# The value multiply of the edge sort on GpSimd instead of VectorE

## The reference

```
x = emb[x_ids]
for each layer:
    h = segment_sum(vals[:, None] * x[col], row)          # sparse times dense
    z = (h + x) @ Wa.T + ba + (h * x) @ Wb.T + bb
    x = where(z >= 0, z, 0.2 * z)
out = concatenate of x before the first layer and after each layer
```

## Time and profile before

| | |
|---|---|
| Median of 3 runs | 10225.11 us (10217.66 to 10225.59) |
| The profiled execution | 10220.25 us, span 10218.3 us |
| Busy share of the span | PE 90%, PE weight load 83%, VectorE 81%, GpSimd 50%, ScalarE 43% |
| Mean granted TensorE clock | 0.92 |
| Sort 0, about | 330 to 1731 us |
| Sort 1, about | 2080 to 3524 us |
| The three layers | from about 3750 us to the end |

### The profile page before, as it was taken

One profiled execution on the slowest core, in us unless ns is written; L12 is line 12 of the kernel. 1 busy time (PEld: TensorE's weight loads), 2 busy tenths in 40 slices (PEclk: granted clock), 3 DMA queues, 4 the chain that ended last, 5 costly groups with the idle time before them and its releaser, 6 DMA issues.

```text
span 10218.3 us, 236191 instructions
## 1 busy us (share of the span) xinstructions
PE 9241.7 (90%) x72184; PEld 8455.2 (83%) x72185; DVE 8226.2 (81%) x11648; ACT 4417.4 (43%) x13845; POOL 5098.6 (50%) x2843
## 2 busy tenths in 40 slices
PE   6788886788888669999999999999999999999999
PEld 4567665466676549999999999989999999999999
DVE  7899998699999857777777777777777777777777
ACT  0577775067777516652111256641111466511112
POOL 8477775057777500006888600028888200088885
PEclk8788887778888759999999999999999999999999
DMA  2111111011111299998888889998888699988885
GB/s 74 35 6 6 6 6 18 6 5 6 6 6 6 23 61 344 344 335 295 284 286 286 252 277 341 340 313 285 286 286 286 224 344 347 336 282 286 286 286 210
DMA packets 1121792, 1969.65 MB, mean 193 GB/s; under 512 B 390740, under 2 KB 442008, under 8 KB 1121080
## 3 DMA queue, kind: packets, MB, share of 16 engines
q0 software_dynamic: 399392, 1034.26, 32.8%
q1 hardware_dynamic: 722328, 934.52, 30.9%
HBM read 1212.58 MB, written 755.66 MB: 193 GB/s over the span
## 4 chain that ended last, share of the span: by engine, by line
PE 48%; DVE 20%; DMA 15%; issue 10%; ACT 3%; SPq 1%; DVEq 1%; POOL 0%; ACTq 0%; POOLq 0%
PE ps L912 35%; DMA messages<-work 14%; PE ps L903 7%; DVE hT L1102 7%; DVE place L1081 7%; DVE hT L1096 3%; ACT work L670 3%; PE ps L746 1%; PE ps L883 1%; PE ps L940 1%; PE ps L920 1%; PE ps L941 1%; PE ps L768 1%; DVE place L1086 0%; DVE place L1084 0%
## 5 line engine op out<-in xcount | busy, mean ns | idle before, releaser
L511 POOL DMA_INDIRECT work<-messages,work x1920 | 2923.1, 1522 | 3687.7 <-issue 3686.8
L912 PE MATMUL ps<-work 128*128 128x125 f32 x30720 | 3548.7, 278 | 38.3 <-DVE work L1279 38.3
L912 PEld LDWEIGHTS ps<-work 128*128 128x128 f32 x30720 | 3504.3, 192 | 82.7 <-DVE work L1279 39.4
L486 POOL DMA_INDIRECT sorted_edges<-stage,run_idx x798 | 1968.5, 2467 | 1286.1 <-ACT stage L615 570.9
L903 PE MATMUL ps<-xb,work 125*128 x21504 | 2459.2, 277 | 149.0 <-DVE work L1251 80.3
L903 PEld LDWEIGHTS ps<-xb,work 125*128 125x128 f32 x21504 | 2425.6, 193 | 182.6 <-issue 182.1
L1279 DVE TENSOR_TENSOR work<-work,iota_p 128x1000 f32<-128x1000 f32 x1920 | 2291.5, 1193 | 34.7 <-ACT work L688 34.7
L670 ACT ACTIVATE work<-ps,work 128x128 f32<-128x128 f32 x5376 | 1515.5, 372 | 1264.9 <-DMA messages<-work 648.5
L688 ACT ACTIVATE work<-work 128x8 f32<-128x8 f32 x1920 | 577.7, 301 | 2880.4 <-DMA work<-messages,work 2880.4
L796 PEld LDWEIGHTS ps<-hT 128*128 128x128 f32 x12768 | 1694.7, 215 | 69.4 <-issue 46.5
L626 ACT ACTIVATE hT<-iota_p,place 128x128 f32<-128x128 f32 x4788 | 1427.9, 386 | 707.7 <-DVE place L1086 699.7
(11 more groups left out here) (201 smaller groups left out, 3820.8 us busy)
## 6 DMA issues: line engine op xcount, KB each, us to landing
messages<-work SPq DMA_DIRECT2D x2688, 256.0 KB, 6.2
work<-slot_cols SPq DMA_DIRECT2D x672, 256.0 KB, 6.0
work<-messages,work POOLq DMA_INDIRECT x1920, 5.9
out_x<-xb SPq DMA_DIRECT2D x150, 125.0 KB
sorted_edges<-stage,run_idx POOLq DMA_INDIRECT x798, 3.7
work<-lane_places SPq DMA_DIRECT2D x532, 5.2 KB
out_x<-xb SPq DMA_DIRECT2D x4, 1562.5 KB
sorted_edges<-hT SPq DMA_DIRECT2D x4, 908.0 KB
```

The costliest lines, as they stand in the source:

```text
L486: pool.indirect_dma_start(out=sorted_edges[p], out_offset=bass.IndirectOffsetOnAxis(ap=run_idx[:, q, k:k + 1], axis=0), in_=stage[:, q, k ...
L511: pool.indirect_dma_start(out=ck[:, n, :, :].rearrange("p h x -> p (h x)"), out_offset=None, in_=octs, in_offset=bass.IndirectOffsetOnAxis ...
L912: last = t.matmul(part[n], ck[:, n, j // CH, j % CH * D:(j % CH + 1) * D], sel[:, n % SELB, j, :], start=j == 0, stop=j == CHB - 1)
```

## The change

GpSimd gets a function `move_values`, which multiplies in_slot by the values into `moved[q][:, :, 1, :]` and signals a new semaphore `valued_ready`. It is issued for window n + 1 ahead of the three scatters of window n. VectorE keeps the multiply by the packed numbers, and waits for `valued_ready` of the window before where it waited for `moved_ready` alone, that is ahead of writing in_slot; TensorE's `order` waits for it too.

```diff
--- before.py
+++ after.py
@@ -303,6 +303,7 @@
         slot_link = sem("slot_link")
         in_slot_ready = sem("in_slot_ready")
         moved_ready = sem("moved_ready")
+        valued_ready = sem("valued_ready")
         act_copies = sem("act_copies")
         parts_link = sem("parts_link")
         parts_ready = sem("parts_ready")
@@ -477,6 +478,13 @@
 
             pool.wait_ge(zero_filled, 9 * DMA)
 
+            def move_values(p, i, q):
+                n = WOFF[p] + i * 2 + q
+                pool.wait_ge(in_slot_ready, n + 1)
+                g.tensor_tensor(out=moved[q][:, :, 1, :], in0=in_slot,
+                                in1=value[p][:, bass.ds(i * (2 * LANES) + q * LANES, LANES)][:, :, None].to_broadcast([P, LANES, SLOTS]),
+                                op=ALU.mult).then_inc(valued_ready, 1)
+
             def scatter(p, i, q, first):
                 pool.wait_ge(stage_ready, WOFF[p] + i * 2 + (q + 1))
                 if not (first and q == 0):
@@ -491,10 +499,19 @@
                     ).then_inc(scattered[p][q], DMA)
 
             for p in range(2):
+                half = WINDOWS[p] // 2
+                move_values(p, 0, 0)
+                move_values(p, 0, 1)
                 scatter(p, 0, 0, True)
+                move_values(p, 1, 0)
                 scatter(p, 0, 1, True)
-                pairs(pool, 1, WINDOWS[p] // 2 - 1, lambda i, q: scatter(p, i, q, False))
-                scatter(p, WINDOWS[p] // 2, 0, False)
+
+                def both(i, q):
+                    move_values(p, i + q, 1 - q)
+                    scatter(p, i, q, False)
+
+                pairs(pool, 1, half - 1, both)
+                scatter(p, half, 0, False)
 
             octs = messages.rearrange("(c h) f -> c (h f)", h=HALVES)
             with pool.Fori(0, LAYERS) as la:
@@ -789,6 +806,7 @@
             def order(p, i, q, first):
                 n = WOFF[p] + i * 2 + q
                 pe.wait_ge(moved_ready, n + 1)
+                pe.wait_ge(valued_ready, n + 1)
                 pe.wait_ge(parts_ready, n + 1)
                 if not first:
                     pe.wait_ge(stage_ready, n - 1)
@@ -1091,17 +1109,16 @@
                 if not first:
                     dve.wait_ge(ordered, n - 1)
                 dve.wait_ge(slot_link, n + 1)
-                if not first:
+                if not (first and q == 0):
                     dve.wait_ge(moved_ready, n)
+                    dve.wait_ge(valued_ready, n)
                 v.tensor_tensor(in_slot, slot[:, :, None].to_broadcast([P, LANES, SLOTS]),
                                 iota_s[:, None, :].to_broadcast([P, LANES, SLOTS]), ALU.is_equal).then_inc(in_slot_ready, 1)
                 v.tensor_tensor(to_part[q][:, ACTL:LANES, :], part_of[:, ACTL:LANES][:, :, None].to_broadcast([P, LANES - ACTL, P]),
                                 iota_p[:, None, :].to_broadcast([P, LANES - ACTL, P]), ALU.is_equal)
                 dve.wait_ge(in_slot_ready, n + 1)
-                for f, field in enumerate((packed[p], value[p])):
-                    last = v.tensor_tensor(moved[q][:, :, f, :], in_slot,
-                                           field[:, bass.ds(w * LANES, LANES)][:, :, None].to_broadcast([P, LANES, SLOTS]), ALU.mult)
-                last.then_inc(moved_ready, 1)
+                v.tensor_tensor(moved[q][:, :, 0, :], in_slot, packed[p][:, bass.ds(w * LANES, LANES)][:, :, None].to_broadcast([P, LANES, SLOTS]),
+                                ALU.mult).then_inc(moved_ready, 1)
 
             def sort(p):
                 half = WINDOWS[p] // 2
```

## The result

| | before | changed |
|---|---|---|
| median | 10223.46 us (10217.66 to 10225.59, 4 runs) | 10038.25 us (10036.78 to 10044.87, 4 runs) |
| ratio | | 0.9821, 95% interval 0.9804 to 0.9838 |
| span of the profiled execution | 10218.3 us | 10043.1 us |

The kernel is 185 us faster; 10,345 was forecast, so the forecast was wrong, and in its sign. The range for 8 in 10 (10,020 to 10,520) holds the measured time, though only because it was drawn to take in rival 1. The layers changed by some 5 us at most: in the last 6603 us of the changed kernel TensorE is busy for 6331 us, in the last 6598 us of the other for 6333. The gain is in the sorts, which from their first reduction to their last take 2774 us together before and 2589 us after.

The account below looks back on a forecast made before the run. VectorE was taken to bound the sorts at 10.51 us a window; GpSimd would then pace them at 8.35 + 2.63 = 10.98, +0.47 over 262 windows, +123 us, forecast 10,345 us. Range for 8 in 10: 10,020 to 10,520.

Parts of the forecast that it names:

- rival 1: In the sorts, GpSimd's multiply does not hold VectorE: about 9.8 us a window, 10,040 us; chance 14%.
- floor of 9.48 us from TensorE: In the sorts, TensorE's matmuls take 2521 us over 266 windows, 9.48 us each, a floor on any gain.
- M: GpSimd's added two-input multiply of 128x1152 f32 per sort window, put at 2.63 us, own range 2.4 to 3.0.
- the walk: Step-by-step timing of one sort window on VectorE and GpSimd: period 8.35 + M = 10.98 us, GpSimd pacing.
- M holds VectorE's two-input instructions: In the sorts, VectorE's two-input instructions wait for all of M from its start; beside the reduction M costs nothing.
- M follows 0.30 later: On GpSimd, M starts 0.30 us after the third scatter ends, at 8.35 us, and ends at 10.98.
- let A be what it held: On VectorE, the one-hot comparison (A, 2.58 us) is the instruction M holds, starting when M ends.
- rival 2: VectorE's small scalar operations are held too; if the first scatter beats the one-hot, period 9.71 us, 10,015 us; chance 4%.
- the stage data come in time: The ordering the walk's first scatter needs is ready at -2.7 us, 3 us early.
- second branch: Rival 2 with the first scatter missing the port and waiting for the one-hot's end: 11.55, +272, 10,495 us; chance 11%.
- Rival 3: M issued over 0.89 us later than 8.35 comes behind the one-hot, all in series: 12.0 us, 10,615 us; chance 12%.
- Rival 4: GpSimd's multiply is short, 1.35 to 2.1 us: period 9.7 to 10.4, -212 to -20 us; chance 5%.

Follow-up runs that it names:

- e_deep_late: Changed kernel with GpSimd's multiply two windows ahead of its scatters and also waiting for VectorE's multiply of the same window: 9945.17 us, ratio 0.9687 to before.
- e_deep: Changed kernel with GpSimd's multiply one window further ahead, that of n + 2 before the scatters of n: 10410.25 us, ratio 1.0182 to before.
- e_add_m: Against the kernel before: VectorE keeps both multiplies, GpSimd repeats the value multiply into a buffer of its own: 10856.01 us, ratio 1.0586.
- e_psum_places: Changed kernel with places and scaled places in PSUM, so no small operation has all its inputs in SBUF: 10157.66 us, ratio 0.9907 to before.
- e_m_second: Changed kernel with GpSimd's multiply of the next window between the first and second scatter instead of ahead of the first: 11087.06 us, ratio 1.0815 to before.
- e_late: Changed kernel with only the wait for VectorE's multiply added before GpSimd's multiply, order kept: 10075.38 us, ratio 0.9815 to before.

## Why the prediction was wrong

**What bounds.** That VectorE set the pace held: with GpSimd's multiply cut to one lane the 1.27 us taken from VectorE shows in full, 9.24 us a window. The floor of 9.48 us from TensorE did not: the best version runs at 9.24. TensorE's mean granted clock was 0.81 to 0.83 in the stretches of the earlier trace rows, and 0.84 when these are kept to the sorts; in the sorts of the changed kernel it was 0.87 and 0.88, in those of e_deep_late 0.90. Its matmuls took 1598.7 + 422.5 + 378.2 = 2399 us in the changed kernel, 9.02 a window, and 2338 us in e_deep_late, 8.79 a window, for the same work. A mean over windows of 7.6 us and windows of 9 to 11 us was used as a constant.

**Removed and added.** 1.27 us from VectorE: right. M = 2.63: the trace draws 2.72, but in the changed kernel that span begins 0.56 us before the end of the scatter in front of it (1007.18 against 1007.74, and 1018.29 against 1018.85), where the walk had a gap of 0.30 behind it. What counts for GpSimd's loop is the time from the scatter's end to the multiply's end: 2.15 us (1007.74 to 1009.89; 2.15 or 2.16 for 262 multiplies), where the walk had 0.30 + 2.63 = 2.93. Where the multiply waited for its semaphore and started 0.08 us behind the scatter, beside the reduction, it took 2.12 us (e_deep_late). From VectorE's side it is 1.93 us (e_deep, 3.28 - 1.35) or 2.28 (e_add_m). Whether the multiply does some of its work under the scatter's tail, or is only drawn from an earlier point, these traces do not tell.

**M holds VectorE's two-input instructions.** Taken as the upper bound, and right: L1120, the one-hot of e_psum_places, one of the two multiplies of e_add_m. The Trainium skill (SBUF — State Buffer, "SBUF: two separate sides") has this as an exclusive lock, and the traces agree. By its second half the scalar operations in a two-port mode take part; L1102, which has one tensor input, was held to 0.05 us after the multiply's end, and was not held when its operands were in PSUM; whether its read or its write in SBUF is what is held was not separated. I had this rule as a rival and not in the walk.

**The walk.** Three of its steps failed. The first is "M follows 0.30 later": M's span starts 0.30 + 0.56 = 0.86 us sooner, and 10.98 - 0.86 = 10.12. (M's 0.09 more and a one-hot that needs 2.53 us after a hold, not 2.66, about cancel.) The second is "let A be what it held". What M holds is L1102, 0.57 us ahead of the one-hot. When M ends the small operations run, and the first scatter, issued 0.17 us after M (1021.17 after 1021.00), gets its index before the one-hot starts at 1021.44; in that place it takes 1.58 us (the row at 1021.17), not 3.78. e_psum_places is the test: with the small operations out of the way the scatter falls behind the one-hot, and the period is 10.13, as the walk has it with its first step mended. With L1102 held, the walk gives rival 2's 9.71 less the same 0.86: an estimate of 8.85 us for GpSimd's loop, less than VectorE's 9.24. GpSimd would then pace nothing, and every window would be 9.24, as in e_deep_late. The third is "the stage data come in time": at a period of 9.24 they do not. A short window's reduction ends 0.24 us after the multiply (1010.13 against 1009.89), so the one before ended 9.00 before it, and the walk's own terms (0.25 and 0.87, and TensorE's window from the experiment with one lane) put the stage data, as an estimate, 0.3 us before the multiply's end behind a TensorE window of 7.6 us, and 2.3 us after it behind one of 10.2. The scatter at 1012.39, behind the latter, started 2.50 us after it. The trace of before held the sign of it: at a period of 10.51 already, the scatter of the earlier trace rows had waited 2.82 us for the stage copy, as 11 of the 45 that waited between 2500 and 3000 us had.

So the forecast's error of 1.19 us a window (10.98 to 9.79) comes apart like this: 0.86 is where GpSimd's multiply falls behind the scatter, which alone turned the sign; 0.89 more (10.13 to 9.24) is the instruction that is held; and 0.55 (9.24 to 9.79) is given back by the late stage copies. One slip is without effect: the 262 windows are 266 less one at either end of each sort, not two.

**The rivals.** Rival 1 had the measured time, 10,040, by luck: VectorE is held, which it denied. Rival 2 was the mechanism, and its first branch, 9.71 us and 10,015, lies 23 us off, with two errors that nearly cancel (0.86 us too long a loop, no late stage copies); it got 4%, since I took the 0.87 us of waking for the gap between a multiply and a scatter that waits for nothing. That gap is 0.17. Its second branch does not occur as such; but the kernel does alternate, between 9.24 and 10.7, through the stage copy that I had put "3 us early": that held at a period of 10.98 and not at 9.24. Rival 3's order, in which in_slot waits for the multiply, is what e_m_second does, at 13.6 us and not 12.0; its threshold of 0.89 us was not tested, and the changed kernel stays clear of it. Rival 4, a short multiply, got 5%: 2.15 us from the scatter's end is what a multiply of 1.85 us behind the walk's gap would give, inside its 1.35 to 2.1.

## What to carry to other kernels

Work moved to GpSimd beside a busy VectorE is priced more by where it falls than by its length: here the same multiply cost nothing (e_deep_late), 1.9 us (e_deep) or 4.4 us a window (e_m_second, 13.6 against 9.24), and both an early and a late one cost. Find the VectorE instruction that does not use two SBUF inputs (here the reduction from PSUM), make GpSimd's work fit in it, give it slack by working a window ahead, and tie its start to the end of the VectorE instruction before, even with a wait that the data does not need. Here it took both: ahead alone was 1.8% slower than before (e_deep), the wait alone changed nothing (e_late). In a walk of two coupled loops, a gap of a few tenths decides which of two patterns closes; where the gaps are unknown, give the patterns like chances.

## What was not expected of the hardware

- GpSimd's two-input multiply ran at 1.7 ns per element ((2718 - 2386) ns over 192), and took 2.12 us for 1152 where it started behind the end of the scatter. The Trainium skill (GPSIMD Engine Reference, "Performance versus the Vector engine") has 4497 ns for 2048, 2.2 ns each. One operand here repeats each value 48 times; whether that is the difference was not tried.
- A multiply behind an indirect DMA on GpSimd shows a start 0.56 us before that DMA's end, while DMA behind DMA shows 0.30 us between them.
- TensorE's mean granted clock was higher where the sort was faster: 0.77 in the sorts of e_add_m (12.8 us a window), 0.84 before, 0.87 to 0.88 changed, 0.90 in e_deep_late. Its time per window fell below what had looked like a floor.
